# Second attention: where TensorE issues a pair's weighted sum

## What is computed

```
xn = x / max(norm(x), 1e-12) * g * sqrt(256)
q, k, v = split(w_qkv @ xn)            # 8 heads of 32
sim = (q * 32**-0.5)^T k               # per image and head 2304 x 2304
out = softmax(sim) v
y = w_out @ out + b_out + x
```

## Time and profile before

| | us |
|---|---|
| three runs | 5220.33, 5223.14, 5220.38 |
| their median | 5220.38 |
| span of the profiled execution (its own time is not listed beside it) | 5216.1 |
| second attention, first to last weighing | 3829 to 5164 |

### The profile page before, as it was taken

One profiled execution on the slowest core, in us unless ns is written; L12 is line 12 of the kernel. 1 busy time (PEld: TensorE's weight loads), 2 busy tenths in 40 slices (PEclk: granted clock), 3 DMA queues, 4 the chain that ended last, 5 costly groups with the idle time before them and its releaser, 6 DMA issues. The chain is left out here.

```text
span 5216.1 us, 112540 instructions
## 1 busy us (share of the span) xinstructions
PE 4171.7 (80%) x32161; PEld 2822.7 (54%) x32161; DVE 4319.4 (83%) x25277; ACT 4144.4 (79%) x6082; POOL 1502.1 (29%) x362
## 2 busy tenths in 40 slices
PE   8576677776776667766777777898999999999999
PEld 4344445444444344444555445443567777777776
DVE  4899899998999899989999999531378888888886
ACT  2798799988998788988999889644267887778785
POOL 0344345443454344444444444200100000000000
PEclk9677777777777677767777777899899999999999
DMA  6000000000000000000000000200320101011112
GB/s 211 6 18 16 7 17 17 8 17 14 11 17 17 7 17 8 17 16 8 17 18 8 17 16 8 65 6 0 151 73 25 35 25 34 25 34 33 26 34 93
DMA packets 79613, 154.90 MB, mean 30 GB/s; under 512 B 8120, under 2 KB 49464, under 8 KB 73528
## 3 DMA queue, kind: packets, MB, share of 16 engines
q1 hardware_dynamic: 78904, 146.72, 9.8%
HBM read 99.50 MB, written 47.19 MB: 28 GB/s over the span
## 5 line engine op out<-in xcount | busy, mean ns | idle before, releaser
L542 POOL TENSOR_TENSOR a_probs<-a_scores,a_probs 128x2304 f32<-128x2304 f32 x288 | 1460.2, 5092 | 1728.3 <-ACT a_probs L465 1728.3
L560 DVE MAX8 a_top<-a_scores 128x8 f32<-128x36 f32 x18432 | 1831.1, 180 | 47.0 <-ACT a_scores L449 47.0
L376 PE MATMUL a_ps_t<-ident,a_probs 128*128 128x128 f32 x5184 | 974.7, 326 | 646.7 <-ACT a_probs_t L460 520.1
L376 PEld LDWEIGHTS a_ps_t<-ident,a_probs 128*128 128x128 f32 x5184 | 673.9, 164 | 934.5 <-ACT a_probs_t L460 656.4
L465 ACT ACTIVATE a_probs<-a_scores,a_steep_kth 128x2304 f32<-128x2304 f32 x290 | 641.2, 2211 | 242.3 <-DVE a_minus_max L696 242.3
L1159 PE MATMUL b_ps_t<-ident,b_soft 128*128 128x128 f32 x5184 | 748.4, 280 | 20.5 <-issue 18.6
L1284 DVE TENSOR_SCALAR_CACHE_REDUCE b_soft<-b_ps_s 128x2304 f32<-128x2304 f32 x288 | 735.3, 2553 | 28.4 <-PE b_ps_s L1143 10.4
L460 ACT ACTIVATE a_probs_t<-a_ps_t 128x512 f32<-128x512 f32 (+1 forms) x1440 | 726.9, 545 | 22.3 <-PE a_ps_t L376 7.9
L1159 PEld LDWEIGHTS b_ps_t<-ident,b_soft 128*128 128x128 f32 x5184 | 583.2, 142 | 205.7 <-issue 80.6
L1241 ACT ACTIVATE b_soft<-b_soft,b_minus_max 128x2304 f32<-128x2304 f32 x288 | 638.1, 2216 | 41.6 <-issue 24.4
L366 PE MATMUL a_ps_s<-a_k_stack,a_q_ring 128*128 128x512 f32 (+1 forms) x1465 | 651.7, 604 | 14.2 <-ACT a_scores L449 9.6
(11 more groups left out here) (134 smaller groups left out, 4149.7 us busy)
## 6 DMA issues: line engine op xcount, KB each, us to landing
a_k_stack<-k_parts SPq DMA_DIRECT2D x72, 288.0 KB, 6.0
b_k_stack<-k_parts SPq DMA_DIRECT2D x72, 288.0 KB, 6.0
a_q_ring<-q_parts SPq DMA_DIRECT2D x294, 64.0 KB
b_q_ring<-q_parts SPq DMA_DIRECT2D x294, 64.0 KB
k_parts<-p_high SPq DMA_DIRECT2D x36, 256.0 KB, 2.1
k_parts<-p_rest SPq DMA_DIRECT2D x36, 256.0 KB, 2.1
q_parts<-p_high SPq DMA_DIRECT2D x36, 256.0 KB, 2.0
q_parts<-p_rest SPq DMA_DIRECT2D x36, 256.0 KB, 2.0
```

Source lines behind the costliest of these rows:

```text
L376: last = pe.transpose(ps_t[(NTG * s + g) % 2][:, P * m:P * m + P], probs[s % 2][:, P * (m0 + m):P * (m0 + m) + P], cst["ident"][:, :])
L542: pool.tensor_tensor(probs[u][:, :], scores_all[:, 2 * (p % 2) + u, :], probs[u][:, :], ALU.subtract).then_inc(masked_ready, 1)
L560: last = dve.max(top8[s // 2 % 2][:, s % 2, c, :], scores_all[:, s % 4, CHUNK * c:CHUNK * c + CHUNK])
```

## The change

PE's `pair_step` issues all five groups of the weighing where it issued the first three, and none later. The instructions, their waits and the other engines' orders stay as they are.

```
                 turn(s, 3, tile)
                 if before > 0:
-                    for g in range(3):
+                    for g in range(NTG):
                         weigh(p - 1, g, pair - 1, h)
                 turn(s, 4, tile)
                 turn(s + 1, 0, tile + 1)
...
                 turn(s + 1, 2, tile + 1)
                 turn(s + 1, 3, tile + 1)
-                if before > 0:
-                    for g in range(3, NTG):
-                        weigh(p - 1, g, pair - 1, h)
                 turn(s + 1, 4, tile + 1)
```

## The result

| us | before | after |
|---|---|---|
| median of four runs | 5221.76 | 5332.58 |
| lowest and highest | 5220.33 to 5226.13 | 5329.02 to 5334.44 |
| span of the profiled execution | 5216.1 | 5330.9 |
| one pair between two loop turns | 9.12 | 9.89 |

The ratio is 1.0212, with a 95% interval of 1.0197 to 1.0226: slower by 110.8 us. The forecast was 5334, the range 5312 to 5357.

A forecast was written before the change was run, and what follows sets the result against it. PE's own work and the chain through ACT's copy and DVE's reduction reach the scores together at +5.05. A pair grows 0.83 us; 135 pairs give 112, loop turns 1.7: 5220.4 + 114 = 5334 us, range 5312 to 5357.

The forecast's parts named there:

- step 1: Between transposes and weighing on PE: one border fewer, with the blocks joined, saves PE 0.22 us a pair.
- step 2: First half of the pair: the joint block stands before the fifth group of transposes and delays it by 0.85 us.
- step 3: Second half: PE waits 0.50 before the fifth group, 0.26 before the next tile's first, 0.30 before scores; sum 1.06 us.
- step 4: From scores to next weighing: 2.63 us, less 0 to 0.05 (0.02 taken) as DVE's reduction of the parts comes sooner.
- step 5: Count over the stage: 135 spaces at 0.83 give 112 us, six loop turns at net 0.28 give 1.7; sum +114.
- A: Second tile's fifth group: waits stay hidden, only the border counts; 31 us off, 5189 us; chance 0.03.
- B: Second half: only ACT's copies cost, scores start at +4.75; 0.55 us more a pair, 5295 us; chance 0.06.
- C: PE's clock falls to 1.2 GHz: half the stage, 5730 us, chance 0.03; small form, one slow stretch per loop turn, 16 us.
- D: Whole pair: border gain and waits balance, no change within about 10 us; chance 0.02.

The follow-up runs named there:

- split23: The kernel before with two groups of the weighing in the first place and three in the second: 5240.69 us, 25.2 over before, 9.37 a pair.
- short_dve: The changed kernel with DVE's reduction over 1536 of 2304 columns: 5294.16 us, 70.1 over the kernel before, 9.65 a pair.
- short_both: The changed kernel with DVE's reduction and ACT's exponentials both over 1536 of 2304 columns: 5277.67 us, 53.6 over the kernel before, 9.57 a pair.
- split41: The kernel before with four groups of the weighing in the first place and one in the second: 5266.53 us, 51.1 over before.
- drop_second: The kernel before with groups 3 and 4 of the weighing, the second place's piece, never done: 5203.44 us, 20.7 below before, 9.04 a pair.

## Why the prediction was right

Step by step, forecast and measured:

- The border (step 1): 0.22 us of PE time saved; the joint block holds PE for 2.28, so 0.99 + 0.08 + 1.44 - 2.28 = 0.23. Right, but no gain: it comes off 1.07 us that stood in a wait, and the 0.84 us that are left of them are now paid.
- The first half (step 2): 0.85 forecast, 2.28 - 1.44 = 0.84 measured. From the run without the second piece (9.04 a pair) to 4 and 1 the block in the first place holds PE 0.42 longer and the pair grows by 0.42, to 5 and 0 by 0.84 and 0.85: this growth is paid in full.
- The waits (step 3): 0.50, 0.26 and 0.30 forecast; 0.49, 0.27 and about 0.33 measured, 0.31 more than before. I had counted 0.22 for the two transposes of the parts, where the scores follow 0.13 behind if nothing holds them. With these, PE's side adds up: 9.12 - 0.23 + 0.49 + 0.27 + 0.31 - 0.07 (step 4) = 9.89. The reason I gave for the first wait, ACT's own order with an exponential ahead of the copies, holds only for a small part: with short exponentials 0.41 of the 0.49 is left. That DVE's chain ends at +5.05 whatever stands in the second place is shown by five kernels that start the scores at +5.04 or +5.05 with 0, 4 and 12 weighing records there.
- From the scores to the weighing (step 4): 2.61 forecast, 2.56 measured, outside my bound of 0.05 under 2.63. I had argued that no idle of PE is shown there. But the idle column can't show it. The eight transposes ahead of the long block took 1.05 us to the block before, against 0.97 after (4604.25 to 4605.22). Before:

```profile
4522.73 1.12 PE L1159 MATMUL b_ps_t<-ident,b_soft 128*128 128x128 f32 x8
4523.78 1.50 PE L1178 MATMUL b_ps_o<-b_soft_t,b_v 128*32 128x256 f32 x24
```

So PE did wait for DVE's copies, under the modelled ends, and the sooner reduction of the parts freed that. The runs bear it out: where DVE adds up the parts 0.37 to 0.40 us behind the start of the scores (before, `split23`, `short_dve`, `short_both`) the eight take 1.05 to 1.09, where it does so 0.06 or 0.07 behind (after, `split41`, `drop_second`) 0.97. So the pair cost 0.77, not 0.83.
- The count (step 5) has the second miss, on the other side. I let PE's earlier end at a loop turn count in full, net 0.28 a turn. Measured between weighing blocks over the six turns it is 14.26 us on average before and 15.54 after, 1.28 each: 0.85 from the block to the fifth group, nothing from there to the branch that closes the loop, 0.10 from the branch until PE resumes, 0.33 from there to the next block. One turn of each kernel, before and after: PE's fifth group, ACT's copy of the third group in the second half, and the branch in the records of PE's sequencer, the part of the engine that waits at semaphores and takes branches.

```profile
4501.15 0.88 PE L1159 MATMUL b_ps_t<-ident,b_soft 128*128 128x128 f32 x6
4504.11 0.59 ACT L1248 ACTIVATE b_soft_t<-b_ps_t 128x512 f32<-128x512 f32 x1
L1226 PEldq COMPARE_BRANCH  x1: 3552/3552/3552, 4504.8 to 4504.8; - x1
```

```profile
4012.14 0.88 PE L1159 MATMUL b_ps_t<-ident,b_soft 128*128 128x128 f32 x6
4015.10 0.59 ACT L1245 ACTIVATE b_soft_t<-b_ps_t 128x512 f32<-128x512 f32 x1
L1223 PEldq COMPARE_BRANCH  x1: 3625/3625/3625, 4015.8 to 4015.8; - x1
```

In both the branch begins about 3.7 us behind the fifth group and takes about 3.6. The sequencer runs ahead of the matmuls: when the last transposes start at 4505.33 before, the branch has been under way for 0.5 us. It begins 0.14 us behind the end of ACT's copy, which frees the bank for the last group, the last wait of the loop's body; with short exponentials that copy ends 0.09 sooner, and the branch begins at +3.60. So PE's end doesn't start the branch, and an earlier end is not passed on. The step should have gone by the branch, not by PE's idle time in the earlier trace rows; that is 0.57 of the 1.00 missed a turn. The other 0.43, a longer branch and a slower stretch behind it, I had at nothing. That stretch takes 3.28 to 5.95 us in the turns of the kernel before: 3.28 where the granted clock stays at 1.00 (4171 to 4175), 5.95 where it shows 0.50. Whether the change itself lengthens it is open.

The misses nearly cancel: -0.06 in some 113 pairs is -7 us, the seven pairs ahead of a change of head grew by 0.54 each (9.47 to 10.01), -2, and the six turns bring +6. The pairs of the last head, written out behind the loop, went from 9.10 to 9.95. From the first weighing block to the last the stage grew from 1334.8 to 1446.7 us, 111.9; I had 114. That it is so close is luck, as the two errors have nothing to do with each other; either one alone, -9 or +6, would have left the time in the range.

The rivals: A (waits hidden) falls with the pair of 9.89 us, where it has 8.90. PE's window shows 138 of 145 us, 0.95 and not the 0.9 forecast, as modelled ends cover part of the waits. B (only ACT's copies) falls with the runs 4 and 1, the short exponentials and the short reductions. C (the clock) doesn't come between loop turns, where it is 1.00; at the turns it falls in both kernels, and the 0.33 us a turn, 2 us in all, is what is seen of its small form. The Trainium skill, TensorE: Matmul & The Clock Gate, "A second HAM failure mode", tells of a kernel whose short idles between groups of matmuls let the clock swing. This trace doesn't show that, with three waits of 0.27 to 0.49 us in every 9.89 and the clock at 1.00. D falls with the result.

## What to carry to other kernels

An engine that is busy all the time need not be the bound: look for a second chain that arrives at the same instant, and ask of each block of work on the busy engine whether it would have waited there anyway. Work that fills such a wait is nearly free where it stands (0.08 of 1.07 us here) and is paid in full elsewhere, so joining two blocks for a cheaper border can lose more than the border. A block left out, as in the run without the second piece, shows in one run what its place is worth. And where an engine's ends are modelled, look for its waits in the distances from start to start, against a run in which nothing holds it: in the changed kernel the idle column showed one of three.

## What the runs showed of the hardware

With two PSUM banks taken in turn, PE waited 0.41 us for a bank although ACT, which copies it out in 0.60, had stood idle for 0.45 before the copy; a shorter exponential took only 0.08 off this wait and nothing off the pair. One border less between 128x128 transposes and 128x32 weighing saved 0.23 us of PE time. And the pause at a loop turn hangs on the sequencer's branch: it began 0.14 us behind ACT's copy that the last group waits for, about 3.7 us behind the fifth group, whether PE's last transposes started at +4.18 or at +3.60.
